# A four-layer cross-attention kernel: VectorE's order in the early layers, and softmax denominators of the last attention from a second PV with ones

## The chip, the cores and the metric

The kernel runs on one core of one Trainium2 chip. The metric is the device time of one execution in microseconds (us), the median of several runs. The engines are TensorE (PE in the profile; PEld is its weight load), VectorE (DVE), ScalarE (ACT), GpSimd (POOL) and SyncE (SP), which issues most of the DMAs.

## The reference, cut to what matters

Eight sequences of 128 rows by 256 columns pass through four cross-attention layers, each against the context `ctx_2048`.

- L0: attention over channels with 16 heads of 8 (Q, K, V from 128x128 weights), then an instance norm: `X = (xn * deviation + mean) * mask`, where the statistics of x itself are taken with the mask.
- L1: 16 heads of 16 over 256 keys (context and latents), RMS norm, MLP of 1024.
- L2: two attentions with 16 heads of 128, then an MLP of 1024.
- L3, the last attention: `softmax(q k^T / 4) v` with 16 heads of 16 and 128 keys, output projection, residual, layer norm, MLP of 1024.

The part of L3 that is changed is this one, per head:

```
w   = exp(s - max(s))          # s = q k^T over 128 keys
out = (w / sum(w)) @ v         # before: w is divided, then multiplied by v
out = (w @ v) / (w @ 1)        # after: both products, then one division
```

## The kernel before, in words

Every engine runs its own written-out program, and all of them walk the same lists of events: `first_order()` for L0 and L1 (events placed at ticks by hand with `put`), `att_order("L3")` for the last attention. The event names are the same on every engine: `S` scores of a unit, `T` transposing its probabilities, `PV`, `OUT` (attention output leaves PSUM), `WO` (output projection), `pq`/`pk` (the stacks of queries and keys for two units), `dq`/`dk`/`dv` (dense projections), `nS`/`nX`/`nT` (norm), `w` (a weight pack split into a high and a low part), `up` (MLP). Semaphores tie them together. TensorE takes most general results in two alternating PSUM banks, so that a late reader of one holds up the product after next.

In L3 there are 4 iterations (two sequences each) of 4 stacks of 2 units, 32 units in all; a unit is four heads of one sequence, a 128x512 block. Per unit: TensorE's scores (L899); VectorE's maximum with the sign turned (L1609); four exponentials on ScalarE, each with a sum over the row through `accum_out` (L1270); VectorE's reciprocal of the four sums (L1560); GpSimd's product of the 128x512 probabilities with them (L1857); the transpose (L909), which waits for `nm`, the product; a copy to SBUF by ScalarE for even units and by VectorE for odd ones (L1281, L1622); and PV (L932), four products of 32 output rows in column groups. `T` of a unit stands 3 units behind its `S`, `PV` 5. At the end of an iteration `OUT` splits 128x512 outputs into high and low parts (ScalarE L1287, VectorE L1625), and `WO` follows two units later.

VectorE does not take the L3 list as it stands: `late` moves the kinds in `LATE["L3"]`, among them `pk` and `OUT`, behind the maximum of the next unit:

```python
        if st == ph and e[0] in kinds and scores[0] < n < scores[-1]:
            kept.append((st, *e))
            continue
        ...
        if st == ph and e[0] == "S":
            yield from kept
```

In L0, `xs` b takes VectorE's statistics of sequence b (two reductions of 128x256, L1533 and L1535), at tick 10b; behind the last of them stand six operations on 128x8 numbers (L1542 to L1547), each of which waits for the one before (`link`). `res` finishes two sequences of L0 (L1772, L1773: two 128x512 operations). In L1, `OUT` stands ahead of `T` of the same tick: VectorE waits in L1625 for ScalarE's copy of the output before it copies an already transposed unit (L1622).

Of the kernel before, what the change touches and what calls it, by code (L numbers as in the profile page):

```python
# [28 lines left out]
P = 128  # L29
# [65 lines left out]
SEAM_COVER = {("nT", "L2nm", 0): 5, ("nT", "L2nm", 2): 6, ("pq", "L3", 0): 6, ("S", "L3", 2): 9}  # L95
# [8 lines left out]
def first_order():  # L104
# [8 lines left out]
    for b in range(B):  # L113
# [26 lines left out]
    for k, (dev, mul, res, lat) in enumerate([(84, 91, 95, 119), (None, 93, 99, 123), (150, 152, 155, 160), (None, 154, 158, 164)]):  # L140
# [30 lines left out]
def att_order(ph):  # L171
# [36 lines left out]
    if ph == "L3":  # L208
        put(6, "nT", "L3n1", 2)
# [214 lines left out]
def build(nc, x, ctx_in, mask_t, mask_s2, mask_s3, packs, cols, rows, l2rows, inds, ident_in, out):  # L424
    stack = ExitStack()
    with stack:
# [81 lines left out]
        vt, o = carve(fs, 0, [2, 2, 2, H, 32])  # L508
        va, o2 = carve(fs, 0, [2, 2, H, 32])
# [33 lines left out]

# [200 lines left out]
        def _(pe):  # L745
# [87 lines left out]
            def prep(ph, e, s, gi, a):  # L833

                it, m = divmod(s, STEPS)
                if s == 0 and e == "pq":
# [10 lines left out]
                if e == "pq":  # L847
# [5 lines left out]
                    j_full(last, (a["stA"], nA * s + 1))  # L853
# [9 lines left out]
                j_full(last, (a["stA"], nA * s + 2 + gi), (a["stD"], nD * s + 1 + gi))  # L863

            def att(ph, e, i, *k):
# [36 lines left out]
                elif e == "T":  # L902
                    pe.wait_ge(a["nm"], i + 1)
# [7 lines left out]
                    last.then_inc(a["tm"], 1)  # L911
                elif e == "PV":
# [24 lines left out]
                elif e == "WO":  # L937
                    pe.wait_ge(a["oeD"], i + 1)
# [242 lines left out]
        def _(act):  # L1181
# [45 lines left out]
            def att(ph, e, i, *k):  # L1227
# [35 lines left out]
                elif e == "S":  # L1263
# [18 lines left out]
                elif e == "OUT":  # L1282
# [155 lines left out]
        def _(dve):  # L1438
# [649 lines left out]
```

## Time and profile before

| | |
|---|---|
| median of 3 runs | 1173.12 us (1172.62 to 1173.24) |
| the profiled execution | 1175.04 us, span of its profile 1173.2 us |
| busy in the span | PE 1062.5 us (91%), DVE 727.7 (62%), ACT 715.2 (61%), POOL 317.5 (27%) |
| mean granted TensorE clock | 0.978 of full speed |
| chain that ended last | PE 66%, DVE 12%, ACT 10%, issue 7%, POOL 2% |

L0 fills about the first 205 us, L1's attention runs to about 360 us, then L1's MLP and both attentions and the MLP of L2; the last attention lies between about 1006 and 1120 us, and its MLP is the rest. A busy share is a mean over stages with different limits: what a change is worth is read from the waits of its own stage. The ends of TensorE's matmuls are modelled and overlap, so the distance of two starts is the better measure of what one costs.

### The profile page before, as it was taken

The numbers are of one execution on the slowest core, as the hardware profiler recorded it, in microseconds if no ns is written. First come the engines' busy times: TensorE is split into PE (matmuls) and PEld (weight loads), VectorE is DVE, ScalarE is ACT, GpSimd is POOL, SyncE is SP. The second block draws the span as 40 slices with busy tenths as digits, with TensorE's granted clock in tenths as the row PEclk, the third lists the DMA queues.
The fourth block names the chain that finished last, engine by engine and source line by source line (L and its number), as shares of the span: only waits on it lengthen the run. The fifth ranks groups of instructions, "written<-read, shape, count | busy, mean of one in ns | idle before, by whom it ended". The sixth has DMA issues, their size and how long they took to land.

```text
span 1173.2 us, 24063 instructions
## 1 busy us (share of the span) xinstructions
PE 1062.5 (91%) x8248; PEld 936.7 (80%) x8248; DVE 727.7 (62%) x1747; ACT 715.2 (61%) x2080; POOL 317.5 (27%) x440
## 2 busy tenths in 40 slices
PE   7998897789978999999998989999999989778788
PEld 5776675677758979999998868999998979667588
DVE  7777574667886645555555645555555585667773
ACT  2776765677884456666655546666665452689852
POOL 5232543756540012211111103111112112143311
PEclk9999899899999999999999999999999999899899
DMA  5211011011101021111001101011111110100100
GB/s 171 66 46 41 22 43 33 15 23 27 45 20 53 19 90 46 46 46 46 19 29 68 46 1 57 35 46 46 46 46 37 37 54 1 48 18 19 48 10 28
DMA packets 29853, 48.09 MB, mean 41 GB/s; under 512 B 6627, under 2 KB 20389, under 8 KB 29734
## 3 DMA queue, kind: packets, MB, share of 16 engines
q1 hardware_dynamic: 29638, 46.49, 12.7%
q8 instruction: 68, 1.11, 0.4%
q14 instruction: 51, 0.42, 0.1%
q10 hardware_dynamic: 96, 0.07, 0.0%
HBM read 36.54 MB, written 1.05 MB: 32 GB/s over the span
## 4 chain that ended last, share of the span: by engine, by line
PE 66%; DVE 12%; ACT 10%; issue 7%; POOL 2%; SPq 1%; DMA 1%; ACTq 0%; DVEq 0%; POOLq 0%
PE ps L764 14%; PE ps L765 14%; PE ps L766 14%; PE ps L1008 4%; PE ps L984 4%; PE ps L1146 3%; ACT pt L1270 2%; PE ps L993 2%; PE ps L909 2%; DVE nm L1806 2%; PE ps L1133 1%; PE ps L1124 1%; PE ps L932 1%; DVE nmax L1609 1%; POOL pt L1857 1%
## 5 line engine op out<-in xcount | busy, mean ns | idle before, releaser
L1857 POOL TENSOR_TENSOR pt<-pt,prec 128x256 f32<-128x256 f32 (+1 forms) x224 | 180.8, 808 | 628.2 <-DVE prec L1678 500.4
L1325 ACT ACTIVATE pt<-ps,nmax 128x129 f32<-128x129 f32 x256 | 92.1, 366 | 101.0 <-DVE nmax L1670 100.2
L764 PE MATMUL ps<-rs 128*128 128x256 f32 x480 | 142.8, 298 | 4.1 <-DVE rs L1692 2.8
L1471 DVE TENSOR_TENSOR rs<-wraw,rs 128x256 fp32r<-128x256 f32 (+2 forms) x116 | 68.8, 595 | 124.5 <-ACT rs L1201 124.1
L765 PE MATMUL ps<-rs 128*128 128x256 f32 x480 | 135.9, 283 | 0.0
L766 PE MATMUL ps<-rs 128*128 128x256 f32 x480 | 135.8, 283 | 0.0
L1270 ACT ACTIVATE pt<-ps,nmax 128x256 f32<-128x256 f32 (+1 forms) x256 | 105.1, 423 | 42.6 <-DVE nmax L1609 42.3
L764 PE MATMUL ps<-ht,rs 128*128 128x256 f32 (+1 forms) x304 | 107.6, 354 | 9.0 <-DVE ht L1521 3.0
L766 PE MATMUL ps<-ht,rs 128*128 128x256 f32 (+1 forms) x304 | 101.4, 333 | 0.0
L765 PE MATMUL ps<-ht,rs 128*128 128x256 f32 (+1 forms) x304 | 101.3, 333 | 0.0
L764 PEld LDWEIGHTS ps<-rs 128*128 128x128 f32 x480 | 91.8, 191 | 7.9 <-DVE rs L1692 4.8
L1692 DVE SCALAR_TENSOR_TENSOR rs<-ps,col,rs 128x256 fp32r<-128x256 f32 x128 | 61.9, 484 | 53.1 <-ACT rs L1342 53.1
L765 PEld LDWEIGHTS ps<-rs 128*128 128x128 f32 x480 | 92.0, 192 | 0.0
L766 PEld LDWEIGHTS ps<-rs 128*128 128x128 f32 x480 | 91.9, 191 | 0.0
L764 PE MATMUL ps<-rs,ct 128*128 128x256 f32 x288 | 86.4, 300 | 3.4 <-ACT rs L1252 1.5
L1806 DVE TENSOR_REDUCE nm<-ps 128x2 f32<-128x512 f32 x128 | 82.1, 679 | 7.0 <-PE ps L1124 7.0
L1609 DVE TENSOR_REDUCE nmax<-ps 128x2 f32<-128x512 f32 (+1 forms) x96 | 65.6, 684 | 29.3 <-PE ps L899 21.9
L984 PEld LDWEIGHTS ps<-fs 128*128 128x128 f32 x512 | 75.7, 190 | 10.1
L1365 ACT ACTIVATE fs<-ps,col 128x256 f32<-128x256 f32 x96 | 40.2, 471 | 68.4 <-PE ps L766 67.3
L1413 ACT ACTIVATE pt<-ps 128x512 f32<-128x512 f32 x128 | 73.1, 599 | 14.2 <-PE ps L1133 12.2
L765 PE MATMUL ps<-rs,ct 128*128 128x256 f32 x288 | 80.9, 281 | 0.0
L766 PE MATMUL ps<-rs,ct 128*128 128x256 f32 x288 | 80.9, 281 | 0.0
(206 smaller groups left out, 2998.8 us busy)
## 6 DMA issues: line engine op xcount, KB each, us to landing
wraw<-in_packs SPq DMA_DIRECT2D x52, 512.0 KB, 3.8
rs<-rs SPq DMA_DIRECT2D x222, 32.0 KB, 1.9
bvr<-in_l2rows SPq DMA_DIRECT2D x16, 256.0 KB, 4.6
rs<-rs SPq DMA_DIRECT2D x96, 16.0 KB
row<-in_rows SPq DMA_DIRECT2D x2, 640.0 KB, 4.9
XH<-in_packs SPq DMA_DIRECT2D x2, 512.0 KB, 4.0
out<-X SPq DMA_DIRECT2D x4, 256.0 KB, 2.1
X<-in_x SPq DMA_DIRECT2D x3, 256.0 KB, 3.3
```

What stands on the lines that cost most here:

```text
L764: nc.tensor.matmul(dst, w[0], m[1], start=start, stop=False)
L765: nc.tensor.matmul(dst, w[1], m[0], start=False, stop=False)
L766: return nc.tensor.matmul(dst, w[0], m[0], start=False, stop=stop)
L984: last = nc.tensor.matmul(ps[:, S_BANK + g % 2, b * D:b * D + P + 1], qT[:, hh % 3, 2 * b2 + b, :], kT[:, hh % 3, 2 * b2 + b, :], start=Tr ...
L1270: last = nc.scalar.activation(prob[:, i % PROBS, h * keys:(h + 1) * keys], ps[:, SCORE_BANKS[ph][i % len(SCORE_BANKS[ph])], h * keys:(h + ...
L1325: last = nc.scalar.activation(prob[:, g % PROBS, k * D:k * D + P + 1], ps[:, S_BANK + g % 2, k * D:k * D + P + 1], ACT.Exp, bias=nmax[:, g ...
L1413: nc.scalar.activation(pt[:, i % L0_PTS, :], ps[:, L0_X[i % len(L0_X)], :], ACT.Exp, scale=Q0_SCALE).then_inc(Z["ex"], 1)
L1471: last = nc.vector.tensor_tensor(dst[1], src, f32(dst[0]), ALU.subtract)
L1609: nc.vector.tensor_reduce(nmax[:, i % 4, 0:nh], ps[:, SCORE_BANKS[ph][i % len(SCORE_BANKS[ph])], :].rearrange("p (h n) -> p h n", h=nh), A ...
L1692: nc.vector.scalar_tensor_tensor(cc[1][:, hd, two, :], ps[:, O_BANK + g % 2, 0:D].rearrange("p (b n) -> p b n", b=2), C(f"L2bv{p // PAIRS ...
L1806: nc.vector.tensor_reduce(nm[:, s % 3, im, 2 * p:2 * p + 2], ps[:, L0_S[i % len(L0_S)], :].rearrange("p (h n) -> p h n", h=2), AX.X, ALU.m ...
L1857: nc.gpsimd.tensor_tensor(pr, pr, prec[:, u % 4, 0:nh].unsqueeze(2).broadcast_to([P, nh, keys]), ALU.mult)\
```

## The change

In L0 the statistics of the sequences 1 to 7 move to the ticks 10, 26, 30, 42, 46, 58 and 62, and the six small operations behind them become six events `xf` at the ticks 74 to 79. `res` is cut into one event for each sequence, two ticks apart. In L1 `T` comes ahead of `OUT`.

In L3:

- the exponentials lose `accum_out`; the reciprocal of the sums and GpSimd's product are gone, and the transpose waits for the exponentials alone (`ex`);
- PV has four more products with the same moving data and a tile `one` as weights, whose 32 columns are 16 ones and 16 zeros (or the reverse), so that each head's sum comes out once for each of its 16 output rows;
- an output bank now belongs to a quarter of four units (two halves: numerators and denominators, 128x256 each). For each of the 8 quarters VectorE takes a reciprocal of 128x256 numbers out of PSUM and a product of the two, ScalarE rounds the quotient to its high part, and GpSimd subtracts to get the low one (`LO`, two units later; for the last quarter at once);
- `WO` comes two units later than before; for the first stack `pk` comes ahead of `pq`, six covering matmuls ahead of `pq` go, and the second `nT` of the norm comes behind `S` 1 instead of ahead of `S` 0.

```diff
-        if b:
-            put(10 * b, "xs", b)
+            put((10, 26, 30, 42, 46, 58, 62)[b - 1], "xs", b)
+    for k in range(6):
+        put(74 + k, "xf", k)
...
-        put(res, "res", k)
+        for half in range(2):
+            put(res + 2 * half, "res", k, half)
...
     if ph == "L3":
+        put(1, "nT", "L3n1", 1)
...
-    for _, e, k in prep:
+    for _, e, k in prep if ph == "L1" else prep[::-1]:
         yield (e, 0, k)
-    if ph == "L3":
-        yield ("nT", "L3n1", 1)
...
             yield ("PV", w // U)
-            if w % per_it == per_it - 1:
-                yield ("OUT", w // per_it)
+        if ph == "L3" and 0 <= w < total and w % 4 == 3:
+            yield ("OUT", w // 4)
+        if ph == "L3" and w >= 4 and (w % 4 == 1 and w < total or w == total - 1):
+            yield ("LO", w // 4 - (w % 4 == 1))
         if ph == "L1" and 0 <= u - T_LAG < total:
             yield ("T", u - T_LAG)
+        if ph == "L1" and 0 <= w < total and w % per_it == per_it - 1:
+            yield ("OUT", w // per_it)
...
-                    pe.wait_ge(a["nm"], i + 1)
+                    pe.wait_ge(a["nm" if ph == "L1" else "ex"], i + 1)
...
+                elif e == "PV" and ph == "L3":
+                    ...
+                    if i >= 8 and i % 4 == 0:
+                        pe.wait_ge(a["rc"], i // 4 - 1)
+                    for den in range(2):
+                        for q in range(4):
+                            last = nc.tensor.matmul(sums(i // 4)[32 * q:32 * q + 32, den, im, :],
+                                                    one[:, m % 2, :] if den else vt[:, it % 2, im, 0, 4 * m + q, :],
+                                                    probT[:, i % 3, q * P:(q + 1) * P], ...)
...
+                elif e == "LO":                                            # ScalarE
+                    act.wait_ge(a["rc"], i + 1)
+                    if i >= 2:
+                        act.wait_ge(a["done"], i // 2)
+                    nc.scalar.copy(uu[0][:, :, i % 2, :], quot[:, i % 2, :, :]).then_inc(a["oeA"], 1)
...
+                elif e == "OUT" and ph == "L3":                            # VectorE
+                    dve.wait_ge(a["pm"], 4 * (i + 1))
+                    link(nc.vector.reciprocal(inv, sums(i)[:, 1, :, :]))
+                    if i >= 2:
+                        dve.wait_ge(a["oeD"], i - 1)
+                    nc.vector.tensor_tensor(quot[:, i % 2, :, :], sums(i)[:, 0, :, :], inv, ALU.mult).then_inc(a["rc"], 1)
...
+                if e == "LO":                                              # GpSimd
+                    pool.wait_ge(a["oeA"], i + 1)
+                    nc.gpsimd.tensor_tensor(uu[1][:, :, i % 2, :], quot[:, i % 2, :, :], uu[0][:, :, i % 2, :].bitcast(F32), ALU.subtract)\
+                      .then_inc(a["oeD"], 1)
```

VectorE in L0, at the statistics of the last sequence (L1533, L1535) and the six small operations. L1806 is the maximum of a block of scores, L1813 adds the running maximum to the queries, L1820 and L1825 normalise an output. Before:

```order
L1825 TENSOR_TENSOR fs<-ps,rcp 128x4x2x8 x4
L1806 TENSOR_REDUCE nm<-ps 128x2 x2
L1533 ISA fs,sd<-X,mt 128x256
L1533 ISA sd 128x1
L1535 ISA fs,sd<-fs 128x256
L1535 ISA sd 128x1
L1542 RECIPROCAL sd<-sd 128x8
L1543 TENSOR_TENSOR mv<-sd 128x8
...
L1547 TENSOR_SCALAR sd<-sd 128x8
L1813 TENSOR_TENSOR rs<-ps,rs 128x256
L1806 TENSOR_REDUCE nm<-ps 128x2 x4
```

The same small operations in the changed kernel, whose lines have other numbers (L1854 is L1806, L1861 is L1813, L1579 to L1589 are L1542 to L1547):

```order
L1854 TENSOR_REDUCE nm<-ps 128x2 x4
L1579 RECIPROCAL sd<-sd 128x8
L1861 TENSOR_TENSOR rs<-ps,rs 128x256
L1552 TENSOR_TENSOR ct<-ps,ct 128x256 x2
L1854 TENSOR_REDUCE nm<-ps 128x2
L1581 TENSOR_TENSOR mv<-sd 128x8
L1854 TENSOR_REDUCE nm<-ps 128x2
L1583 TENSOR_TENSOR sd<-sd 128x8
L1868 RECIPROCAL rcp<-ps 128x16
L1873 TENSOR_TENSOR fs<-ps,rcp 128x4x2x8 x4
L1854 TENSOR_REDUCE nm<-ps 128x2
L1585 TENSOR_TENSOR sd<-mv 128x8
```

The statistics have moved up by eight ticks, and between two of the small operations there now stands at least one maximum.

TensorE at the head of L3, behind the first `dq`: L851 is `pq`, L858 and L861 are `pk`, L798 is `nT`, L899 is `S`. Before:

```order
L851 MATMUL ps<-rs,sel 128x256 x4
L858 MATMUL ps<-rs,sel 128x256 x2
L861 MATMUL ps<-mb,indr 128x256
L798 MATMUL ps<-ident,XH 128x128 x4
L899 MATMUL ps<-rs 128x256 x2
L851 MATMUL ps<-rs,sel 128x256 x4
L858 MATMUL ps<-rs,sel 128x256 x2
L861 MATMUL ps<-mb,indr 128x256
L899 MATMUL ps<-rs 128x256 x4
```

And now (L864 is `pq`, L871 and L874 are `pk`, L811 is `nT`, L912 is `S`):

```order
L871 MATMUL ps<-rs,sel 128x256 x2
L874 MATMUL ps<-mb,indr 128x256
L864 MATMUL ps<-rs,sel 128x256 x4
L912 MATMUL ps<-rs 128x256 x2
L864 MATMUL ps<-rs,sel 128x256 x4
L871 MATMUL ps<-rs,sel 128x256 x2
L874 MATMUL ps<-mb,indr 128x256
L912 MATMUL ps<-rs 128x256 x2
L811 MATMUL ps<-ident,XH 128x128 x4
L912 MATMUL ps<-rs 128x256 x2
```

The norm's transpose now follows the second unit's scores.

VectorE inside L3, around the maxima of the units 13 and 14: L1609 is the maximum, L1560 the reciprocal of four sums, L1606 the copy of `pk`, L1471 a low part of a weight pack, L1578 `dq`. Before:

```order
L1622 COPY pt<-ps 128x512
L1609 TENSOR_REDUCE nmax<-ps 128x4
L1560 RECIPROCAL prec<-psums 128x4
L1625 TENSOR_TENSOR rs<-ps,rs 128x512
L1606 CAST rs<-ps 64x2x128
L1471 TENSOR_TENSOR rs<-wraw,rs 128x256
L1609 TENSOR_REDUCE nmax<-ps 128x4
L1560 RECIPROCAL prec<-psums 128x4
L1578 SCALAR_TENSOR_TENSOR rs<-ps,col,rs 128x256 x2
```

And now (L1651, L1648, L1507 and L1620 are L1609, L1606, L1471 and L1578):

```order
L1664 COPY pt<-ps 128x512
L1651 TENSOR_REDUCE nmax<-ps 128x4
L1667 RECIPROCAL fs<-ps 128x256
L1670 TENSOR_TENSOR fs<-ps,fs 128x256
L1648 CAST rs<-ps 64x2x128
L1507 TENSOR_TENSOR rs<-wraw,rs 128x256
L1651 TENSOR_REDUCE nmax<-ps 128x4
L1620 SCALAR_TENSOR_TENSOR rs<-ps,col,rs 128x256 x2
```

The division of a quarter (L1667, L1670) stands between a maximum and the copy of the next stack's keys; this pair comes once in four units, behind every second stack.

## Rows read from the trace of the kernel before

**Rows 1.** Windows: stretch and length, busy us of PE, PEld, DVE, ACT, POOL; clock; DMA

```profile
0.00:360.00 360.00, 306.34 (x2623) 241.85 (x2623) 254.63 (x608) 243.23 (x593) 165.00 (x230) 0.96 0.18 48
...
1006.00:1120.00 114.00, 88.41 (x788) 72.52 (x787) 78.30 (x184) 91.22 (x351) 41.14 (x41) 0.94 0.13 34
...
1068.00:1092.00 24.00, 21.84 (x210) 17.74 (x209) 16.44 (x41) 20.65 (x89) 8.90 (x10) 1.00 0.15 37
```

**Rows 2.** Timeline, L0: start, us, engine, line, operation, [idle before, releaser]

```profile
101.58 1.54 DVE L1533 CUSTOM_DVE_ANT_0 fs<-X,mt 128x256 f32<-128x256 f32 x1
...
105.93 0.50 PE L1124 MATMUL ps<-rs 128*128 128x512 f32 x1 [2.17 <-DVE nm L1806]
```

**Rows 3.** Timeline, DVE and PE in the second attention (L1)

```profile
220.95 1.51 DVE L1772 TENSOR_TENSOR X<-X,fs 128x512 f32<-128x512 f32 x1 [1.24 <-POOL X L1945]
...
225.06 0.72 PE L858 MATMUL ps<-rs,sel 128*128 128x512 f32 x2 [2.19 <-DVE rs L1571]
...
256.64 0.69 DVE L1625 TENSOR_TENSOR rs<-ps,rs 128x512 fp32r<-128x512 f32 x1 [1.49 <-ACT rs L1287]
...
258.03 0.64 PE L932 MATMUL ps<-pt,fs 128*32 128x128 f32 x16 [1.11 <-issue]
```

**Rows 4.** Timeline, PE and DVE at the head of the last attention (L3)

```profile
1013.75 0.72 PE L851 MATMUL ps<-rs,sel 128*128 128x256 f32 x4 [2.11 <-DVE rs L1578]
...
1018.71 1.29 DVE L1609 TENSOR_REDUCE nmax<-ps 128x4 f32<-128x512 f32 x2
...
1021.80 0.76 PE L899 MATMUL ps<-rs 128*128 128x256 f32 x2 [3.00 <-ACT rs L1262]
```

**Rows 5.** Timeline, PE: one PV of L1, then one unit of L3

```profile
301.72 0.64 PE L932 MATMUL ps<-pt,fs 128*32 128x128 f32 x16
...
1060.91 0.40 PE L899 MATMUL ps<-rs 128*128 128x256 f32 x2
1061.15 0.60 PE L909 MATMUL ps<-ident,pt 128*128 128x128 f32 x4
1061.68 0.42 PE L932 MATMUL ps<-pt,fs 128*32 128x128 f32 x8
1062.04 0.38 PE L764 MATMUL ps<-rs 128*128 128x256 f32 x1
1062.26 0.28 PE L765 MATMUL ps<-rs 128*128 128x256 f32 x1
1062.38 0.28 PE L766 MATMUL ps<-rs 128*128 128x256 f32 x1
```

**Rows 6.** Timeline, ACT: an exponential of L3, its accumulator, the next

```profile
1064.74 0.37 ACT L1270 ACTIVATE pt<-ps,nmax 128x128 f32<-128x128 f32 x1 [0.68 <-DVE nmax L1609]
1065.00 0.19 ACT L1270 ACTIVATION_READ_ACCUMULATOR pt<-ps,nmax 128x1 f32 x1
1065.09 0.36 ACT L1270 ACTIVATE pt<-ps,nmax 128x128 f32<-128x128 f32 x1
```

**Rows 7.** Groups by line and form, DVE and POOL: busy us, mean ns, idle before

```profile
L1813 DVE TENSOR_TENSOR rs<-ps,rs 128x256 fp32r<-128x256 f32 x32 | 13.3, 417 | 31.8 <-PE ps L1114 31.8
...
L1560 DVE RECIPROCAL prec<-psums 128x4 f32<-128x4 f32 x32 | 5.4, 168 | 3.5 <-ACT pt L1270 3.5
...
L1820 DVE RECIPROCAL rcp<-ps 128x16 f32<-128x16 f32 x16 | 4.0, 248 | 5.7 <-PE ps L1156 5.7
...
L1542 DVE RECIPROCAL sd<-sd 128x8 f32<-128x8 f32 x1 | 0.2, 202 | 0.0
...
L1885 POOL TENSOR_TENSOR X<-X,row 128x256 f32<-128x256 f32 x48 | 38.7, 809 | 75.6 <-ACT fs L1365 75.6
```

**Rows 8.** Timeline, PE in the tail of the last attention

```profile
1112.13 0.36 PE L764 MATMUL ps<-ht,rs 128*128 128x256 f32 x1 [1.76 <-DVE X L1631]
...
1119.52 0.43 PE L932 MATMUL ps<-pt,fs 128*32 128x128 f32 x8 [2.31 <-DVE pt L1622]
...
1121.84 0.41 PE L764 MATMUL ps<-rs 128*128 128x256 f32 x1
```

More of the change, by code:

```diff
@@ L139, in first_order @@
     put(121, "w", "L1sel1")
[L140 removed]
+    for k, (dev, mul, res, lat) in enumerate([(84, 91, 95, 119), (None, 93, 99, 123), (150, 152, 155, 160), (None, 154, 159, 164)]):
         if dev:
@@ L508, in build @@
         vt, o = carve(fs, 0, [2, 2, 2, H, 32])
+        one, o2 = carve(fs, o, [2, 32])
+        inv, o2 = carve(fs, o2, [2, P])
+        quot, o2 = carve(fs, o2, [2, 2, P])
+        assert o2 <= 6168
         va, o2 = carve(fs, 0, [2, 2, H, 32])
@@ L911, in att @@
                     last.then_inc(a["tm"], 1)
+                elif e == "PV" and ph == "L3":
+                    it, r = divmod(i, 2 * STEPS)
+                    m, im = divmod(r, 2)
+                    copied(pe, ph, i)
+                    if r == 0:
+                        pe.wait_ge(a["vals"], it + 1)
+                    if i >= 8 and i % 4 == 0:
[4 more added lines that the diff above has]
+                                                    one[:, m % 2, :] if den else vt[:, it % 2, im, 0, 4 * m + q, :],
+                                                    probT[:, i % 3, q * P:(q + 1) * P],
+                                                    start=i % 4 == 0 and den == 0, stop=m % 2 == 1, skip_group_check=True)
+                    last.then_inc(a["pm"], 1)
                 elif e == "PV":
@@ new lines, in x_stats @@
+                link(nc.vector.tensor_tensor_reduce(ms[:, 0, b, :], X[:, b, :], mt8[:, b, :], 1.0, 0.0, ALU.mult, ALU.add,
+                                                    sd[:, 3, b:b + 1]))
+                last = nc.vector.tensor_tensor_reduce(ms[:, 1, b, :], ms[:, 0, b, :], ms[:, 0, b, :], 1.0, 0.0, ALU.mult, ALU.add,
+                                                      sd[:, 4, b:b + 1])
+                if b == B - 1:
+                    link(last)
+                else:
+                    last.then_inc(l0stat, 1)
@@ new lines, in x_factors @@
+            def x_factors(k):
+                if k == 0:
+                    link(nc.vector.reciprocal(sd[:, 2, :], sd[:, 2, :]))
+                elif k == 1:
+                    link(nc.vector.tensor_tensor(mv[:, :, 0], sd[:, 3, :], sd[:, 2, :], ALU.mult))
+                elif k == 2:
+                    link(nc.vector.tensor_tensor(sd[:, 4, :], sd[:, 4, :], sd[:, 2, :], ALU.mult))
+                elif k == 3:
+                    link(nc.vector.tensor_tensor(sd[:, 5, :], mv[:, :, 0], mv[:, :, 0], ALU.mult))
+                elif k == 4:
+                    link(nc.vector.tensor_tensor(sd[:, 4, :], sd[:, 4, :], sd[:, 5, :], ALU.subtract))
+                else:
+                    nc.vector.tensor_scalar(sd[:, 0, :], sd[:, 4, :], 0.0, None, ALU.max).then_inc(l0stat, 2)
```

77 lines of the change are left out of this document (35 added, 42 removed).

## The prediction, made before the changed kernel ran

> **What bounds the kernel now.** I read the windows by stage first, then for the two stages that the change touches TensorE's timeline with its idle times, and then VectorE's and ScalarE's timelines around each of them. L0 and L1 fill 360 us, in which PE is busy 306 us and DVE and ACT 255 and 243; the last attention fills 114 us with PE 88, ACT 91 and DVE 78 [rows 1]. No engine is full in either: a unit's data goes PE, DVE, ACT, PE, and each engine takes its list in order, so that a time is lost where one engine's list holds an operation that is not ready, or a long one, ahead of what another engine waits for. A change there is worth what it takes out of TensorE's idle times, since TensorE's work is what has to be fitted in (TensorE stands still 54 of the 360 us and 26 of the 114). Inside the last attention the limits differ: from 1068 to 1092 us PE is busy 21.84 of 24 us at full clock, so only 2.2 us are free there; ACT has 20.65 [rows 1].
>
> My sum is made against the profiled execution (span 1173.2 us, its own time 1175.04); the timed runs lie 1.9 us below it with a median of 1173.12. A difference worked out in the trace is carried over to that median as it is.
>
> **L0.** The statistics of the last sequence start at 101.58 us, where the first pass takes 1.54 us, and with the six chained operations they hold VectorE until the next maximum; TensorE then stands 2.17 us, until 105.93, for that maximum [rows 2]. In the new order the pieces lie between maxima, each with one or two small operations, and the passes are placed two ticks behind a group of maxima. The work stays; only its clumping goes. What hides the pieces is that VectorE has some 30% of its time free here; if that cover were gone, the idle time would only be cut up. I take -1.8 us (bounds 0 and -3).
>
> **L1, `res`.** VectorE waits 1.24 us in its order for GpSimd, then needs 1.51 us for the first 128x512 pass, and TensorE's `pk` waits 2.19 us for the `dq`/`dk` piece queued behind [rows 3]. With one sequence at a time the same wait is followed by half of the passes, and maxima of two units come between the halves. I take -1.2 us (bounds 0 and -2.5); eight more instructions cost their start-up alone, some 0.1 us each, and are in it.
>
> **L1, `T` ahead of `OUT`.** At 256.64 VectorE has waited 1.49 us for ScalarE's part of `OUT` and then takes 0.69 us, while a transposed unit lies ready; TensorE's PV starts at 258.03 after 1.11 us of idle [rows 3]. The same pattern stands at the ends of two more iterations, with the same 1.11 and 1.12 us. Now the copy comes first and fits into the wait. The maximum behind it then starts 0.6 us earlier as well. Three times 0.6 us is -1.8 (bounds 0 and 3 x 1.11).
>
> **Head of L3.** `pq` waits 2.11 us for the low part of `dq`; then `nT` stands ahead of the first scores on TensorE, and on VectorE its two passes ahead of the first maximum, which starts at 1018.71; the third unit's scores wait 3.00 us, until 1021.80, for ScalarE, whose `pk` copy is queued behind the exponentials of unit 0 [rows 4]. Now `pk` fills the wait for `dq`, and the maximum of unit 0 can follow its scores at about 1016.5. The exponentials of unit 0, and all behind them, move up by that: -2.5 us (bounds -1 and -3). The six covering matmuls lay in an idle time and free nothing; whether the clock suffers without them is among the doubts below.
>
> **Inside L3.** Four terms.
> - PE gains 4 products in each of 32 PVs. A PV of L1, which has 8 products, takes 0.64 us, one of L3 with 4 takes 0.42 [rows 5]: +0.22 us each, 7.0 us of work.
> - ACT: an exponential's accumulator record starts 0.26 us behind it, the next exponential 0.35 us behind [rows 6]: without it 0.09 us less for each of 128, so 11.5 us less work, 0.36 us a unit. Nearly all of that counts only where ScalarE ends last.
> - DVE loses 32 reciprocals of 0.17 us and four `OUT`s of 0.69 [rows 3, 7], and gains for each of 8 quarters a reciprocal of 256 numbers a row and a product. No row has such a reciprocal. Those of 4 and 16 numbers take 168 and 248 ns, 6.7 ns a number; drawn out to 256, that is 1.85 us. The ends are 0.42 us, if it streamed like the product of 128x256, and 2.31 us, by the step of 34 ns from 4 to 8 numbers [rows 7]. I take 1.85, since the slope over twelve numbers is the nearest row. With the product, 0.42 us, a quarter costs 2.27 us, 18.2 us in all, against 8.2 us removed.
> - POOL loses its 32 products and the wait of the transposes for them. With a lag of 3 units that wait is hidden inside the loop, so I count it at nothing there.
>
> Where the division stands decides. On VectorE it follows the maximum of unit u+1, and behind it is queued the copy of `pk`, for which the scores of u+2 wait. From the start of the scores of u+1 that copy is ready after about 0.3 (scores), 0.65 (maximum, half of 1.29 in [rows 4]), 2.37 (division with its link) and 0.43, some 3.8 us. TensorE meanwhile has scores 0.24, transpose 0.53, PV 0.36 and 0.22, and twelve dense products at 0.12 us, 2.8 to 2.9 us in all [rows 5]. So 0.9 us shows where one dense group follows (the quarters divided behind the units 9, 13 and 21), nothing where `dv` and the moved `WO` both follow (17 and 25), and about 0.5 us at 29, where ScalarE's table loads hold the stage anyway: +3.2 us. From units 16 to 31 PE's extra work finds little room: 3.5 us more against 2.2 us free in 24 us, of which waits for `dq` will keep a part: +1.3 us. Before that ScalarE ends last more often, and I let its relief bring back 3.2 us of its 11.5 (a fourth). Inside L3: +1.3 us.
>
> **Tail.** Of the idle time of 1.76 us at 1112.13, the wait for the add behind the third `WO`, nothing should be left, since `WO` now comes later, and VectorE no longer waits for the last exponentials before it takes the norm's passes. But ahead of the copy of unit 31, for which PE waited 2.31 us already [rows 8], VectorE now has a division and that add: I keep -1.2 us of the gain. After the last PV the old kernel began `WO` 2.3 us later (1119.52 to 1121.84), its `OUT` hidden by a dense group. Now there follow one on another PV's second half 0.2, reciprocal 1.85, product 0.42, ScalarE about 0.4 (its 128x128 pass takes 0.37, [rows 6]), GpSimd 0.81 [rows 7], and hops between engines, 4.3 us from the start of PV: +2.0. Tail: +0.8 us.
>
> **The sum.** -1.8 - 1.2 - 1.8 - 2.5 + 1.3 + 0.8 = -5.2 us, from 1173.12 to 1167.9 us.
>
> **The rivals.**
> - The divisions stop the pipeline (slower). If TensorE's work between the scores of u+1 and u+2 is itself late (its dense group waits for ScalarE or VectorE), the cover of 2.8 us is not there, and each of six inner quarters costs all of 2.4 us and not 0.5 on the mean: +11 us, 1179 us. The wait of `pk` for a long VectorE operation is what the rows of L1 show with `res` (2.19 us idle behind a clump of 2.5 us), so the mechanism is real here; against it, after two of the six there are two dense groups. It decides from 1.4 us a quarter on, where 5.2 us are used up.
> - The early edits bring nothing (no change). L0 and L1 lose 4.8 us in my sum only if no other wait takes the place of those removed; with several engines near 70% that can happen. Then 1172.7 us.
> - ScalarE's relief lies on the path (more gain). If a third of the 11.5 us counts on top and PE's 7.0 us go into its 26 us of idle time, the inner term is -3.8 instead of +1.3: 1162.8 us.
> - A reciprocal that streams (0.42 us): the exposed 3.2 us and 1.4 us of the tail go, 1163.3 us. One at the upper end, 2.31 us, adds 0.46 us at three quarters and in the tail: 1169.7 us, within the forecast's own range.
>
> **How the numbers follow.** About 0.2% (2.3 us) is what a measurement of this kernel can tell from no change. Forecast, 1165 to 1170.8: 0.45. More gain, by ScalarE or a cheap reciprocal: 0.20. Early edits for nothing: 0.18. Divisions that stop the pipeline: 0.17, of which a few are so mild that they end within 0.2%. The range for 8 in 10 is 1161.5 to 1176.5 us. Faster 0.67, same 0.17, slower 0.16.
>
> **What would show each step.** In L0, no idle time of TensorE over about 1.5 us near 106 us; at the three ends of iterations in L1, PV without the 1.11 us; in L3 the first maximum some 2 us after `pq` and no wait of 3 us at the third unit; PV groups of 0.64 us; exponentials 0.26 us apart; a reciprocal of 128x256 near 1.85 us, and behind it waits of TensorE's scores for `pk`, at units 10, 14 and 22 but not 18 and 26; in the tail, TensorE idle about 2 us before the last `WO`. The prediction is wrong if those waits come at all six quarters or reach 2 us, if the dense group's PSUM bank is held up by a late VectorE reader, or if the granted clock of the last attention (0.94 now, [rows 1]) moves, since the idle time before the last `WO` may lower it for the MLP's start.

## The result, and the profile after

The changed kernel takes 1176.51 us (median of 7 runs, 1175.42 to 1177.93), the kernel before 1172.62 us beside it (7 runs, 1170.76 to 1173.58): ratio 1.0036, interval 1.0026 to 1.0047. It is 3.9 us slower, where the forecast was 5.2 us faster, and the median lies 0.01 us above the upper end of the stated range (1176.5). The medians and ratios of this document leave out two disturbed runs, both of e9, which took 1697.45 and 2031.97 us.

The profiled execution of the changed kernel took 1176.4 us (span 1174.6). That is only 1.4 us more than the profiled one of before, which lay 2.4 us above its own median. I therefore compare stages from their own starts. The same three windows after [rows 1]:

```profile
0.00:360.00 360.00, 309.98 (x2661) 246.27 (x2662) 260.63 (x626) 246.81 (x597) 163.77 (x230) 0.96 0.18 48
1006.00:1120.00 114.00, 91.65 (x1002) 75.85 (x1004) 79.93 (x146) 81.40 (x224) 11.74 (x15) 0.93 0.10 25
1068.00:1092.00 24.00, 20.50 (x245) 16.82 (x243) 16.49 (x29) 16.39 (x49) 1.16 (x2) 1.00 0.16 40
```

ScalarE has lost 10 us of work in the last attention and GpSimd 29, and TensorE, with more to do, is busy for less of the window from 1068 to 1092 us: 20.50 us where it had 21.84. Its time now goes into waits.

The early part went mostly as forecast. Timelines of the changed kernel, `res` in L1, then the first `dq` of L3 and its first scores:

```profile
218.97 1.25 DVE L1820 TENSOR_TENSOR X<-X,fs 128x256 f32<-128x256 f32 x1 [1.23 <-POOL X L1999]
...
222.56 0.71 PE L871 MATMUL ps<-rs,sel 128*128 128x512 f32 x2 [1.67 <-DVE rs L1613]
...
1004.46 0.36 PE L777 MATMUL ps<-ht,rs 128*128 128x256 f32 x1 [0.60 <-DVE rs L1620]
...
1009.63 0.80 PE L912 MATMUL ps<-rs 128*128 128x256 f32 x2 [0.78 <-ACT rs L1280]
...
1010.46 0.69 DVE L1651 TENSOR_REDUCE nmax<-ps 128x4 f32<-128x512 f32 x1 [2.01 <-PE ps L912]
```

TensorE's wait behind `res` fell from 2.19 to 1.67 us [rows 3]; the idle time of 2.17 us near 106 us and the three of 1.11 us before PV are gone [rows 2, 3]. The first `dq` of L3 that waits for VectorE starts at 1004.46 us, where it started at 1009.98. The first maximum came to 1010.46 from 1018.71 [rows 4], 2.3 us behind `pq`. One new wait came with it: in L0 one sequence's `res` (L1820 and L1821, from 149.29 us on) now stands ahead of a maximum, and TensorE waits 1.92 us for that. It is in the trace of every kernel with the early edits; the kernel before has a wait of 1.06 us there, for another operation.

```profile
150.10 1.38 DVE L1821 TENSOR_TENSOR X<-X,mt 128x256 f32<-128x256 f32 x1
151.40 0.68 DVE L1854 TENSOR_REDUCE nm<-ps 128x2 f32<-128x512 f32 x1
...
152.23 0.67 PE L1152 MATMUL ps<-rs 128*128 128x512 f32 x1 [1.92 <-DVE nm L1854]
```

All of that, and more, is lost from there on: from the first scores of L3 to the end of the span it was 157.2 us (1016.02 to 1173.2) and is 165.0 us (1009.63 to 1174.6). The starts of scores show where. From unit 8 to 16: 25.0 us before, 24.3 after; 16 to 24: 21.6 and 25.5; 24 to 29: 12.0 and 15.7; from 31 to the last `WO`: 16.4 and 18.4. The timeline around unit 17 of the changed kernel (TensorE, VectorE and ScalarE):

```profile
1058.04 0.40 PE L912 MATMUL ps<-rs 128*128 128x256 f32 x2
...
1058.48 0.69 DVE L1651 TENSOR_REDUCE nmax<-ps 128x4 f32<-128x512 f32 x1 [0.98 <-PE ps L912]
...
1059.09 1.75 DVE L1667 RECIPROCAL fs<-ps 128x256 f32<-128x256 f32 x1
...
1059.38 0.39 PE L777 MATMUL ps<-rs 128*128 128x256 f32 x1
...
1060.87 0.43 DVE L1670 TENSOR_TENSOR fs<-ps,fs 128x256 f32<-128x256 f32 x1
1061.32 0.43 DVE L1648 CAST rs<-ps 64x256 fp32r<-64x256 f32 x1
...
1061.90 0.36 PE L777 MATMUL ps<-rs,ct 128*128 128x256 f32 x1 [0.84 <-DVE rs L1648]
...
1063.40 0.40 PE L912 MATMUL ps<-rs 128*128 128x256 f32 x2
...
1063.84 0.69 DVE L1651 TENSOR_REDUCE nmax<-ps 128x4 f32<-128x512 f32 x1 [1.63 <-PE ps L912]
...
1064.45 0.68 DVE L1679 TENSOR_TENSOR X<-ps,X 128x512 f32<-128x512 f32 x1
...
1064.57 1.14 ACT L1303 ACTIVATE pt<-ps,nmax 128x128 f32<-128x128 f32 x4 [3.75 <-DVE nmax L1651]
...
1065.17 0.75 DVE L1517 BATCH_NORM_STATS2 st<-X 128x6 f32<-128x256 f32 x2
...
1065.28 0.71 PE L864 MATMUL ps<-rs,sel 128*128 128x256 f32 x4 [0.46 <-DVE X L1679]
...
1065.84 0.87 DVE L1634 TENSOR_TENSOR fs<-ps,row 128x128 f32<-128x128 f32 x4
...
1066.85 0.48 PE L871 MATMUL ps<-rs,sel 128*128 128x256 f32 x2 [0.86 <-DVE fs L1634]
...
1067.29 0.40 PE L912 MATMUL ps<-rs 128*128 128x256 f32 x2
```

Read it by the bank. TensorE does `WO` at 1059.38 and then wants the PSUM bank that `pk` wrote, for `dv` (L777 `rs,ct`). VectorE's copy of `pk` out of that bank (L1648) stands behind the division, so `dv` begins at 1061.90 and the scores of unit 18, behind `dv` on TensorE, at 1063.40: 5.36 us after those of unit 17, where it was 2.67. Then the moved `WO` makes a second stall: its add (L1679) and statistics (L1517) and the copy of `dv` (L1634), 2.3 us together, stand on VectorE ahead of what `pq` and `pk` wait for, and unit 19 comes 3.89 us after unit 18 (2.57 before). The same pair stands at unit 25 (5.35 and 4.01 us, where it was 2.65 and 3.09). The move has a return: the intervals that `WO` left, S 15 to S 16 and S 23 to S 24, are 1.0 us shorter each (1.68 and 1.69, where it was 2.66 and 2.65).

The tail of the changed kernel:

```profile
1119.69 0.65 PE L935 MATMUL ps<-pt,fs 128*32 128x128 f32 x16 [2.78 <-DVE pt L1664]
...
1120.40 1.76 DVE L1667 RECIPROCAL fs<-ps 128x256 f32<-128x256 f32 x1 [0.77 <-PE ps L935]
...
1122.20 0.42 DVE L1670 TENSOR_TENSOR fs<-ps,fs 128x256 f32<-128x256 f32 x1
1122.65 0.40 ACT L1317 CAST rs<-fs 128x256 fp32r<-128x256 f32 x1 [5.50 <-DVE fs L1670]
...
1123.14 0.72 POOL L1921 TENSOR_TENSOR rs<-fs,rs 128x256 fp32r<-128x256 f32 x1 [4.65 <-ACT rs L1317]
...
1123.91 0.39 PE L777 MATMUL ps<-rs 128*128 128x256 f32 x1 [1.96 <-POOL rs L1921]
```

From the last PV to the last `WO` it is 4.22 us (2.32 in [rows 8]); the forecast chain is there step by step.

### The profile page after: what moved, and what is told of

Its sections match the earlier page's. It is cut to its first block, busy times and chain, and to the rows that moved or that the text cites. A ratio compares the mean times of both kernels' runs of the same rounds, so it can differ in the third digit from the quotient of the medians.

```text
span 1174.6 us, 24400 instructions
## 1 busy us (share of the span) xinstructions
PE 1069.9 (91%) x8504; PEld 944.7 (80%) x8504; DVE 737.0 (63%) x1735; ACT 707.2 (60%) x1956; POOL 289.8 (25%) x420
## 4 chain that ended last, share of the span: by engine, by line
PE 66%; DVE 14%; ACT 8%; issue 7%; POOL 2%; SPq 1%; DMA 1%; ACTq 0%; DVEq 0%; POOLq 0%
PE ps L777 14%; PE ps L778 13%; PE ps L779 13%; PE ps L1036 4%; PE ps L1012 4%; PE ps L1174 3%; PE ps L1021 2%; PE ps L922 2%; DVE nm L1854 2%; DVE nmax L1651 1%; PE ps L1161 1%; PE ps L1152 1%; POOL pt L1905 1%; ACT pt L1301 1%; PE ps L811 1%
## 5 line engine op out<-in xcount | busy, mean ns | idle before, releaser
L1905 POOL TENSOR_TENSOR pt<-pt,prec 128x256 f32<-128x256 f32 (+1 forms) x192 | 147.5, 769 | 562.3 <-DVE prec L1726 500.0
L777 PE MATMUL ps<-rs 128*128 128x256 f32 x480 | 142.4, 297 | 6.0 <-DVE rs L1740 2.8
L1507 DVE TENSOR_TENSOR rs<-wraw,rs 128x256 fp32r<-128x256 f32 (+2 forms) x116 | 67.8, 586 | 124.3 <-ACT rs L1229 123.9
L777 PE MATMUL ps<-ht,rs 128*128 128x256 f32 (+1 forms) x304 | 108.0, 355 | 7.1 <-DVE ht L1557 3.0
L777 PEld LDWEIGHTS ps<-rs 128*128 128x128 f32 x480 | 91.2, 190 | 9.8 <-DVE rs L1740 4.8
L777 PE MATMUL ps<-rs,ct 128*128 128x256 f32 x288 | 86.4, 300 | 3.5 <-DVE rs L1648 1.7
L1854 DVE TENSOR_REDUCE nm<-ps 128x2 f32<-128x512 f32 x128 | 82.7, 681 | 8.4 <-PE ps L1152 8.2
L1651 DVE TENSOR_REDUCE nmax<-ps 128x2 f32<-128x512 f32 (+1 forms) x96 | 65.8, 685 | 35.3 <-PE ps L912 29.3
L1449 ACT ACTIVATE pt<-ps 128x512 f32<-128x512 f32 x128 | 73.2, 599 | 13.5 <-PE ps L1161 11.5
L1301 ACT ACTIVATE pt<-ps,nmax 128x256 f32<-128x256 f32 x128 | 59.9, 477 | 33.0 <-DVE nmax L1651 32.8
```

The lines of the kernel that those rows point to most:

```text
L777: nc.tensor.matmul(dst, w[0], m[1], start=start, stop=False)
L1301: last = nc.scalar.activation(p_h, s_h, ACT.Exp, bias=nmax[:, i % 4, h:h + 1], accum_out=psums[:, i % 4, h:h + 1])
L1449: nc.scalar.activation(pt[:, i % L0_PTS, :], ps[:, L0_X[i % len(L0_X)], :], ACT.Exp, scale=Q0_SCALE).then_inc(Z["ex"], 1)
L1507: last = nc.vector.tensor_tensor(dst[1], src, f32(dst[0]), ALU.subtract)
L1651: nc.vector.tensor_reduce(nmax[:, i % 4, 0:nh], ps[:, SCORE_BANKS[ph][i % len(SCORE_BANKS[ph])], :].rearrange("p (h n) -> p h n", h=nh), A ...
L1854: nc.vector.tensor_reduce(nm[:, s % 3, im, 2 * p:2 * p + 2], ps[:, L0_S[i % len(L0_S)], :].rearrange("p (h n) -> p h n", h=2), AX.X, ALU.m ...
```

## The experiments

My theory after the result: (A) what costs is where the division stands on VectorE, ahead of `pk`, whose copy frees a PSUM bank and feeds scores, made worse by the moved `WO`; the rival (B) is that the divisions cost by their work on VectorE wherever they stand, or that the other edits (TensorE's more products) do it. The table has every run. "To the changed kernel" is the difference of the ratios times 1172 us; "from S 0" is the time from the first scores of L3 to the end of the span in the one profiled execution (157.2 before, 165.0 changed). It takes in the MLP behind the last `WO`, where the granted clock differs between executions and with it 1 to 2 us of the time (last section).

| run | edit | median us | ratio to the kernel before | to the changed kernel | from S 0 |
|---|---|---|---|---|---|
| changed | | 1176.51 | 1.0036 (1.0026 to 1.0047) | | 165.0 |
| e1 | L0 and L1 edits alone | 1167.26 | 0.9961 (0.9949 to 0.9973) | -8.8 | 156.7 |
| e2 | e1 and the head of L3 | 1165.94 | 0.9948 (0.9936 to 0.9959) | -10.3 | 155.4 |
| e3 | `WO` two units earlier | 1172.84 | 1.0003 (0.9993 to 1.0013) | -3.9 | 162.5 |
| e4 | `pk` ahead of the division | 1170.21 | 0.9974 (0.9962 to 0.9987) | -7.3 | 158.8 |
| e5 | both | 1168.35 | 0.9962 (0.9950 to 0.9974) | -8.7 | 158.8 |
| e6 | no division | 1165.13 | 0.9940 (0.9927 to 0.9953) | -11.3 | 157.4 |
| e7 | `accum_out` back | 1176.43 | 1.0026 (1.0016 to 1.0035) | -1.2 | 165.9 |
| e8 | products with ones twice | 1176.17 | 1.0033 (1.0020 to 1.0046) | -0.4 | 165.7 |
| e9 | e5, division in halves | 1169.62 | 0.9970 (0.9958 to 0.9982) | -7.7 | 159.1 |
| e10 | e5, no division | 1161.75 | 0.9900 (0.9885 to 0.9916) | -15.9 | 151.9 |
| e11 | no division at units 17, 25 | 1171.76 | 1.0001 (0.9991 to 1.0011) | -4.1 | 162.0 |
| e12 | no division at 9, 13, 21, 29 | 1171.60 | 0.9995 (0.9985 to 1.0006) | -4.8 | 161.8 |
| e13 | e10, `accum_out` back | 1164.53 | 0.9946 (0.9933 to 0.9960) | -10.5 | 154.4 |
| e14 | e2, `pk` ahead of `OUT` | 1165.80 | 0.9958 (0.9945 to 0.9970) | -9.1 | 156.1 |

**The parts of the change apart (e1, e2).** e1 is the kernel before with the hunks for `xs`, `xf`, `res` and L1's `T` ahead of `OUT`; e2 adds those of the head:

```diff
+        put(1, "nT", "L3n1", 1)
-    for _, e, k in prep:
+    for _, e, k in prep if ph == "L1" else prep[::-1]:
```

> The kernel before with the edits of L0 and L1 alone (statistics and factors, res in halves, T ahead of OUT); the last attention is the old one. If the early edits give what the traces show at the first dq of L3 (1009.98 to 1004.46), the time is 5 us below the kernel before, ratio 0.9957 (0.994 to 0.997). If they bring nothing, 1.000 within 0.001. The difference between the two then prices the change of the last attention: with 5 us gained early, L3 lost 9 us; with nothing gained early, L3 lost only 4 us.

> As the first, and the head of L3 as changed (pk ahead of pq for the first stack, no covering matmuls ahead of pq, second nT behind S 1), with the old PV, sums and products. If the head edit is worth what its sum says, 2.5 us below the first, ratio to the kernel before 0.9936 (0.992 to 0.9955). If the old wait moves to the next one (the third unit waits for ScalarE, whose pk copy is behind exponentials), it is within 0.5 us of the first.

The early edits bring 4.6 us together; no run takes the three apart. The head brings 1.5 more by the ratios, whose intervals overlap. In the traces it is 2.4 us, from the first `dq` of L3 that waits for VectorE to the end (163.0 us in e1, 160.6 in e2); from S 0 only 1.3 of it shows, since the head's edit also brings S 0 closer to that `dq`. So the rest, the new inside and tail of L3, costs 10.3 us in the medians and 9.6 in the traces, where the prediction had 2.1.

**`WO` back (e3).**

```diff
-            if w == (it + 1) * per_it + ((4 if ph == "L3" else 1) if it + 1 < c["iters"] else 0):
+            if w == (it + 1) * per_it + ((2 if ph == "L3" else 1) if it + 1 < c["iters"] else 0):
```

> The changed kernel with WO two units earlier (behind the units 15, 23 and 31, where the kernel before has it) and nothing else. Theory A (the moved WO and dv stand on VectorE behind the division at the units 17 and 25, and dv's PSUM bank waits for the pk copy behind that division): most of 2 x 4 us comes back, 1168 to 1171 us, ratio 0.993 to 0.996 to the changed kernel, and S 17 to S 18 takes about 2.7 to 3.8 us in place of 5.4. Theory B (the divisions alone cost, wherever WO stands): at most 1 us, ratio 0.999 to 1.000, and S 17 to S 18 stays over 4.5 us.

It gave 3.9 us, between the two theories' figures. The second stall is gone (S 18 to S 19 is 2.57 us again), but S 17 to S 18 is still 4.09: with one dense group behind it, the division alone ahead of `pk` costs 1.4 us there.

**`pk` first (e4) and both (e5).** In `late`, for VectorE alone:

```diff
         if st == ph and e[0] == "S":
+            if ph == "L3":
+                kept.sort(key=lambda e: e[1] == "OUT")
             yield from kept
```

> The changed kernel with VectorE taking the pk copy ahead of the division in each of the quarters (the order of one pair of operations, six places), nothing else. Theory A (what hurts is pk and the PSUM bank behind the division): 7 to 10 us come back, 1167 to 1170 us; S 13 to S 14 and S 17 to S 18 back to 2.7 us. Theory B (the length of VectorE's list is what counts, 2.2 us of division in a stage in which the engines are near full): the time moves by under 2 us, since now the next maximum is behind the division in place of pk.

> The changed kernel with both edits: pk ahead of the division on VectorE, and WO two units earlier. Theory A (two separate queues on VectorE: pk behind the division, and WO's add and statistics with dv at the units 18 and 26): the second's 1.3 us at each of S 18 to S 19 and S 26 to S 27 go as well, and S 17 to S 18 falls from 4.3 to about 2.7: 1165 to 1168 us, 2 to 5 us below the one with pk first. Theory B (they are the same stall, which one of the edits has already taken): 1170 us, as with pk first alone.

The edit puts `OUT` behind everything that `late` holds back, so in these six places the division moves behind the copy of `pk` and behind the low part of a weight pack (L1509). e4 gave 7.3 us for that. Its timeline, VectorE and TensorE behind unit 17 (L1650 is the copy of `pk`):

```profile
1057.14 0.40 PE L914 MATMUL ps<-rs 128*128 128x256 f32 x2
...
1057.58 0.69 DVE L1653 TENSOR_REDUCE nmax<-ps 128x4 f32<-128x512 f32 x1 [0.98 <-PE ps L914]
...
1058.30 0.43 DVE L1650 CAST rs<-ps 64x256 fp32r<-64x256 f32 x1
1058.76 0.43 DVE L1509 TENSOR_TENSOR rs<-wraw,rs 128x256 fp32r<-128x256 f32 x1
1059.22 1.76 DVE L1669 RECIPROCAL fs<-ps 128x256 f32<-128x256 f32 x1
...
1061.43 0.40 PE L914 MATMUL ps<-rs 128*128 128x256 f32 x2
...
1063.31 0.71 PE L866 MATMUL ps<-rs,sel 128*128 128x256 f32 x4 [0.46 <-DVE X L1681]
...
1064.88 0.48 PE L873 MATMUL ps<-rs,sel 128*128 128x256 f32 x2 [0.86 <-DVE fs L1636]
```

The copy is done at 1058.73 and no bank waits: TensorE goes from scores to scores in 4.29 us, all of it work, since `WO` and `dv` both stand in this unit (my expectation of 2.7 us left that out). S 13 to S 14 is 2.87 us, near the 2.79 of the kernel before. The second stall is untouched. In e5 the division makes one of its own in its place:

```profile
1057.57 1.76 DVE L1669 RECIPROCAL fs<-ps 128x256 f32<-128x256 f32 x1
...
1058.10 0.39 PE L914 MATMUL ps<-rs 128*128 128x256 f32 x2
...
1059.36 0.42 DVE L1672 TENSOR_TENSOR fs<-ps,fs 128x256 f32<-128x256 f32 x1
...
1059.70 0.68 DVE L1653 TENSOR_REDUCE nmax<-ps 128x4 f32<-128x512 f32 x1
...
1061.32 0.47 PE L873 MATMUL ps<-rs,sel 128*128 128x256 f32 x2 [1.14 <-DVE fs L1636]
```

The scores of unit 18 lie ready at 1058.5, their maximum comes at 1059.70, `dv`'s copy behind it, and `pk` waits 1.14 us for that. Whether e5 beats e4 stays open: it is 1.9 us in the medians, but the intervals overlap. The traces from S 0 agree only in sum. Up to the last `WO` e5 is 1.7 us ahead (107.4 and 109.1 us), and it loses as much behind it, where both do the same work. From the last `WO` to the end, e4 and then e5 (columns as in [rows 1]):

```profile
1118.89:1168.59 49.70, 44.92 (x368) 43.98 (x368) 26.95 (x51) 16.89 (x36) 8.23 (x8) 1.00 0.06 22
```

```profile
1113.62:1164.97 51.35, 46.76 (x368) 46.00 (x368) 27.04 (x51) 16.91 (x36) 8.22 (x8) 0.95 0.07 21
```

**The parts priced (e6 to e8).** Each is one line of the changed kernel: the reciprocal becomes a copy (the division is left out), the exponentials get `accum_out` back, and the loop over the two kinds of products makes the second twice (the sums come out twice as large).

```diff
-                    link(nc.vector.reciprocal(inv, sums(i)[:, 1, :, :]))
+                    link(nc.vector.tensor_copy(inv, sums(i)[:, 1, :, :]))
...
-                    for den in range(2):
+                    for den in (0, 1, 1):
```

> The changed kernel with the reciprocal replaced by a copy of the same 128x256 numbers out of PSUM (the division is left out, so the quotients are products). It prices the length of the reciprocal. The copy should take 0.4 to 0.5 us in place of 1.75. Theory A (the length of what stands ahead of pk is what stops TensorE): about 1.3 us less at six inner quarters and in the tail, 7 to 9 us in all, 1167 to 1170 us, with S 13 to S 14 at 2.8 us. Theory B (the places of WO and of the dense groups matter, whatever the division takes): S 17 to S 18 stays over 4.5 us and at most 4 us come back.

> The changed kernel with accum_out back on the exponentials of the last attention (their sums are written and not read). It prices ScalarE's relief, 0.09 us for each of 128 and 11.5 us of work. If a fourth of it lies on the path, as the prediction had it, 3.2 us slower than the changed kernel, ratio 1.0027. If VectorE and TensorE now end last nearly everywhere, under 1 us. If it was what the change really brought, over 6 us.

> The changed kernel with the four products with ones made twice in each PV (the sums come out twice as large and the output half). It adds another 0.22 us of TensorE work to each of 32 units, 7.0 us. The prediction let 1.3 us of the first 7.0 us show. If this second dose shows in full, 7 us slower than the changed kernel, TensorE bounds the stage; if 1 to 3 us show, the products are mostly hidden in waits for VectorE.

The division's length is worth 11.3 us by the ratios, above what either theory gave, and 7.6 from S 0 in the traces. The group rows of the changed kernel and of e6:

```profile
L1667 DVE RECIPROCAL fs<-ps 128x256 f32<-128x256 f32 x8 | 14.0, 1749 | 0.8 <-PE ps L935 0.8
```

```profile
L1667 DVE COPY fs<-ps 128x256 f32<-128x256 f32 x8 | 3.3, 415 | 0.8 <-PE ps L935 0.8
```

Eight operations shorter by 1.33 us are 10.7 us of VectorE's work, so seven tenths or more of it was on the path. In e6's profiled execution L0 also ended 3 to 4 us earlier than in most others (last section); how much of the 3.7 us between the two figures is that, I can't say. Not all of the time freed could be used: unit 10's scores now reach the next limit and wait for a DMA of key rows, for which no scores of unit 10 waited in the changed kernel.

```profile
1034.00 0.39 PE L912 MATMUL ps<-rs 128*128 128x256 f32 x1 [1.22 <-DMA rs<-rs]
```

In the times the accumulators and the doubled products cost nothing that shows: 11.5 us of ScalarE's work and 7.0 us of TensorE's. In e8's trace six of the intervals between scores do grow, by 0.21 to 0.23 us each, and from unit 8 to 29 it takes 66.7 us where the changed kernel takes 65.5. So TensorE's products are mostly hidden, not wholly.

**The division in halves (e9), and left out of the repaired order (e10).** `OUT` becomes two events, the second one unit later.

```diff
-            yield ("OUT", w // 4)
+            yield ("OUT", w // 4, 0)
+        if ph == "L3" and w >= 4 and (w % 4 == 0 and w < total or w == total - 1):
+            yield ("OUT", w // 4 - (w % 4 == 0), 1)
```

> The kernel with pk first and WO earlier, and each quarter's division cut into two of 128x128: the first behind pk in the same place, the second behind the next maximum and behind that place's dense copies. Theory A (a long operation ahead of the next maximum and of dv's copy is what is left): a maximum waits at most 0.9 + 0.2 us in place of 2.2, and 2 to 3 us come back: S 18 to S 19 from 3.65 to about 3 us, 1165 to 1166.5 us. Theory B (VectorE's total work decides): the work is the same, with 0.1 us more per piece: 1168 to 1169.5 us.

> The kernel with pk first and WO earlier, with the reciprocal replaced by a copy (the division is left out). It gives what the order can't repair. If the order has already hidden the division, at most 1.5 us less than with the reciprocal (1167 to 1168.5 us). If the length still counts, about 1.3 us at two or three of the quarters and at the last one: 1163 to 1166 us.

Halving brought nothing. S 18 to S 19 fell from 3.65 to 2.72 us, further than expected, but S 10 to S 11 grew from 4.24 to 5.62, and units 8 to 29 take 60.7 us (60.8 in e5). The rows of e9 in that interval say why it grew:

```profile
1039.51 0.29 DVE L1675 TENSOR_TENSOR fs<-ps,fs 128x128 f32<-128x128 f32 x1
...
1039.83 0.40 ACT L1321 CAST rs<-fs 128x256 fp32r<-128x256 f32 x1 [0.83 <-DVE fs L1675]
...
1040.88 0.66 PE L815 MATMUL ps<-ident,XH 128*128 128x128 f32 x4 [1.53 <-ACT rs L1284]
```

The second half of the quotient comes late for ScalarE's `LO`, whose place was not moved; the copy of `pq` (L1284) is queued behind `LO`, and TensorE waits 1.53 us for it (0.58 in e5). The wait for the DMA at unit 10 is also 0.4 us longer than in e5. So e9 doesn't show that VectorE's work as such decides: halves with `LO` moved as well were not tried. e10 then gives what the order doesn't repair: 6.6 us below e5, and 1161.75 us is below the 1163 to 1166 that I had expected. From S 0 it is 6.9 us, of which 5.3 lie ahead of the last `WO`. The other 1.6 lie behind it, where no division stands: e10 ran at full clock there (49.74 us), e5 at 0.95. e4 and e9, which have the division, ran at full clock there too, so these 1.6 us can't be put down to the division.

**Place by place (e11, e12).** The copy in place of the reciprocal at some quarters, the quotients of these being left out:

```diff
-                    link(nc.vector.reciprocal(inv, sums(i)[:, 1, :, :]))
+                    link((nc.vector.tensor_copy if i in (2, 4) else nc.vector.reciprocal)(inv, sums(i)[:, 1, :, :]))
```

> The changed kernel with the reciprocal replaced by a copy at the quarters 2 and 4 alone, whose divisions stand behind the maxima of the units 17 and 25 (there the quotients are left out). The prediction counted these two places at nothing. Theory A (dv's PSUM bank waits for pk behind the division, and the moved WO's work for VectorE piles up behind it): two places of six give back more than half of what lies inside, 3 to 5 us, and S 17 to S 18 falls from 5.4 to about 4. Theory B (the prediction's own account: only places with one dense group show): under 0.5 us.

> The changed kernel with the reciprocal replaced by a copy at the quarters 0, 1, 3 and 5 (units 9, 13, 21 and 29). The prediction counted these places at 3.2 us. Theory A: 1 us each where the waits show in the trace, 3 to 4 us. Theory B (each division costs the stage its whole length, wherever it stands): 4 x 1.3 = 5.2 us here and 2.6 us in the other run.

The two places that the prediction had at nothing are worth 4.1 us, within the 3 to 5 of theory A, the four others 4.8, between A's 3 to 4 and B's 5.2. From the scores of unit 8 to those of unit 29 each run saves 2.0 to 2.1 us in its trace: 1.0 us for each of the two, 0.7 for each of the three of the others that lie there. At the units 9, 13 and 21 themselves it is 0.93 to 0.96 us each (3.81 to 2.88 us at 9), but S 10 to S 11 takes 0.7 us of that back, with 0.54 us of waiting for the DMA of key rows. The fourth shortens S 29 to S 30 from 5.27 to 3.92 us. S 17 to S 18 fell only to 4.30 us, the length of the work that stands there now.

**Two last questions (e13, e14).**

> The kernel without divisions, with pk first and WO earlier (1161.75 us), and accum_out back on the exponentials. If ScalarE's relief was only hidden behind the divisions, 2 to 4 us of its 11.5 show now: 1164 to 1166 us, ratio to the kernel before 0.992 to 0.994. If it lies beside other work in any case, under 1 us: 0.990 to 0.991.

> The kernel with the early and the head edits and the old attention inside (ratio 0.9948), and VectorE taking pk ahead of OUT, which there is a pass of 0.69 us at three ends of iterations. If it is the length ahead of pk that counts, this one is short and covered: no change, 0.994 to 0.996. If any operation ahead of pk stops TensorE, 0.7 us at each of three places: about 0.993.

Without the divisions the accumulators cost 2.5 us from S 0 in the traces (1.9 of it up to the last `WO`), 2.8 in the medians and 5.4 by the ratios (the kernel before was 2.4 us apart in the two groups of runs): ScalarE's relief is real there, some sixth to a half of 11.5, and in the changed kernel the divisions hide it. In the old attention (e14) the order of `pk` and `OUT` is worth nothing: a pass of 0.69 us ahead of `pk` is covered, one of 2.2 us is not.

## Why the prediction was wrong, point by point

- **L0, `res`, `T` ahead of `OUT`**: -4.8 forecast, -4.6 measured (e1, interval -3.2 to -6.0). The sum is right and the rival that they bring nothing is out; the three terms were not measured apart, and the new wait of 1.92 us at 152 us was not foreseen.
- **Head of L3**: -2.5 forecast, -1.5 by the ratios and -2.4 in the traces from the first `dq`. The mechanism was right. The wait that followed was a DMA of key rows in the third unit (0.60 us) and `pq`'s ScalarE copy, not in the sum.
- **The step that failed** is "nothing where `dv` and the moved `WO` both follow (17 and 25)". I set the division against the sum of TensorE's work up to the next scores and found it covered by two dense groups. But the second group could not start: it needs the PSUM bank whose reader, the copy of `pk`, stands behind the division. So the cover was not work beside the division but work queued behind it. TensorE took 5.36 us in place of 2.67. Part of that is the moved work (4.29 us without any wait in e4), part the bank (1.1 us, e11), and behind it the clump of `WO`'s add, statistics and `dv`'s copy gave 1.3 us more. The prediction named the bank among its doubts and priced it nowhere. `WO`'s move, which I counted only in the tail, costs 3.9 us (e3). Beside e2, whose head is the same, the six intervals that the division and the moved `WO` touch here (from 15, 17, 18, 23, 25 and 26) are 5.8 us longer together, of the 9.6 from S 0; the tail from S 31 to the last `WO` has another 2.4.
- **Units 9, 13 and 21**: 0.9 us each forecast; S 13 to S 14 grew by 1.02 us and S 21 to S 22 by 1.16; S 9 to S 10, long before already (4.28 us), did not grow, yet its division holds it too: 3.81 us against 2.88 where it is left out (e12). The forecast's chain of 3.8 us from the scores to the copy of `pk` is the measured 3.81, so the reasoning was right where its cover was free to run. At 29 it is 1.35 us (e12) and not 0.5.
- **ScalarE's relief, -3.2**: nothing in the changed kernel (e7), where the intervals inside are held by VectorE. It is the second term that failed: 3.2 us of the 9.1 between forecast and result. It is 1.9 to 5.4 us where the division is left out (e13). The size was right for a kernel that doesn't exist: I added a gain on one engine to a loss on another on whose path it lay.
- **TensorE's products, +1.3**: the times show nothing of a second dose (e8); in the traces it shows 0.2 us at six intervals, 1.3 us together, and the first dose the same at four (S 5 to S 6, for one, 2.87 us where it was 2.64).
- **Tail, +0.8**: +2.0 from S 31 to the last `WO`, as its chain said; the -1.2 did not come, since PV of unit 31 now waits 2.78 us for VectorE where it waited 2.31 [rows 8].

The result is near the rival "the divisions stop the pipeline". Its price of 2.4 us at each of six places was too high and its condition not general (0.7 to 1.4 us a place by e11, e12 and S 29 to S 30, plus what `WO` adds), but with the relief at nothing that was enough.

The fastest kernel that computes the reference is e2: 1165.94 us, 0.9948 of the kernel before (0.9936 to 0.9959); e14 is no different from it. The products with ones would pay only with a cheaper division: e10 lies 4.2 us below e2 without any (5.6 by the ratios).

## What to carry to other kernels

Before a long operation's cover is summed up, check for each piece of the cover which buffer it needs and where that buffer's last reader stands: a PSUM bank read behind the long operation turns cover into queue. Don't add a relief on one engine to a new stall on another of the same loop; price it with the stall in place. And sums that are copied to 16 rows so that no broadcast is needed make the division 16 times as wide: 1.75 us for a quarter, where four reciprocals of four numbers took 0.17 us each [rows 7].

## What the runs showed that I had not expected

The time of L0 differs by 3 to 4 us between executions of the same instructions, and the granted clock goes with it. The window from 120 to 180 us of the changed kernel and then of e6, whose L0 is the same:

```profile
120.00:180.00 60.00, 51.87 (x426) 40.97 (x423) 44.53 (x106) 41.23 (x74) 26.27 (x47) 0.94 0.15 39
```

```profile
120.00:180.00 60.00, 51.45 (x458) 40.03 (x457) 45.52 (x108) 42.73 (x77) 28.32 (x52) 1.00 0.14 39
```

The last scores of L0 start at 180.3 us in the first and at 176.1 in the second, which got 458 products into the window at a granted clock of 1.00 instead of 426 at 0.94. The profiled execution of e5 had 1.00 there too, and came to the last scores of L0 at 176.9; those of the changed L0 with 0.91 or 0.94 came to them between 178.4 and 180.6. The same holds at the other end. From the last `WO` to the end the kernels with the new attention take 49.7 us in the traces that have full clock there (e4, e9, e10) and 50.7 to 51.4 where 3.4 to 4.8 us of it ran at half clock (the changed kernel, e3, e5, e7, e8, e11, e12). So a difference of 2 us between two traces says nothing until both are set to the start of the stage and the clock of the stage is the same.
